# Four side-by-side products of 32 output columns in place of one of 128 in a softmax attention

## What is computed

```
qkv = (x @ W_qkv + b_qkv).reshape(B, S, 3, H, hd)
q, k, v = (qkv[:, :, 0], qkv[:, :, 1], qkv[:, :, 2])
attn = jnp.einsum('bqhd,bkhd->bhqk', q, k) / jnp.sqrt(jnp.asarray(hd, x.dtype))
attn = jax.nn.softmax(attn, axis=-1)
attn_out = jnp.einsum('bhqk,bkhd->bqhd', attn, v).reshape(B, S, D)
```

## Time and profile before

| | us |
|---|---|
| median of three runs | 2016.27 (2015.23 to 2020.01) |
| the profiled execution, device time | 2018.79 |
| its span in the profile | 2017.1 |
| PE busy | 1833.6 (91%), 10746 matmuls |
| DVE busy | 1480.3 (73%) |
| ACT busy | 939.5 (47%) |
| POOL busy | 965.1 (48%) |
| `pass_attend` | about 1563 to 2016 |

### The profile page before, as it was taken

How to read it: one execution, slowest core, us unless ns; L and a number is a source line. 1 busy time by engine, 2 the same in 40 slices (tenths; PEclk the granted TensorE clock), 3 DMA queues, 4 the chain that set the end, 5 groups by cost and what they waited for, 6 DMA issues and landing times. The chain is left out here.

```text
span 2017.1 us, 36263 instructions
## 1 busy us (share of the span) xinstructions
PE 1833.6 (91%) x10746; PEld 1204.9 (60%) x10746; DVE 1480.3 (73%) x4020; ACT 939.5 (47%) x2132; POOL 965.1 (48%) x1658
## 2 busy tenths in 40 slices
PE   6997997999899999799999699599799699999997
PEld 5886774444688888577777333388677233333332
DVE  3334896777477777699998498577798589998981
ACT  1112564666121121344443244355444477777777
POOL 3554564666333333233333111088743776666663
PEclk9997998999799999899999799699899699999999
DMA  4330668887100000695000200067786344443320
GB/s 134 117 117 27 163 167 207 162 173 144 48 1 1 1 1 1 270 413 232 1 1 1 65 10 10 29 157 200 193 254 204 69 107 101 102 106 92 88 68 28
DMA packets 241706, 215.01 MB, mean 107 GB/s; under 512 B 117210, under 2 KB 216188, under 8 KB 241404
## 3 DMA queue, kind: packets, MB, share of 16 engines
q1 hardware_dynamic: 227804, 183.51, 34.1%
q0 software_dynamic: 9408, 25.70, 3.9%
q10 hardware_dynamic: 4320, 3.70, 0.7%
HBM read 108.04 MB, written 103.12 MB: 105 GB/s over the span
## 5 line engine op out<-in xcount | busy, mean ns | idle before, releaser
L2918 ACT ACTIVATE attend_w<-ps 128x512 f32<-128x512 f32 x512 | 279.9, 598 | 91.2 <-PE ps L2785 67.1
L3121 DVE TENSOR_REDUCE attend_mx<-ps 128x1 f32<-128x512 f32 x448 | 281.7, 682 | 36.1 <-PE ps L2773 26.5
L2785 PE MATMUL ps<-keep_o,keep_x 99*128 99x512 bf16 x512 | 191.9, 384 | 2.4 <-ACT attend_w L2918 2.4
L2773 PE MATMUL ps<-keep_x,keep_o 96*128 96x512 bf16 x448 | 173.3, 387 | 8.0 <-DVE attend_mx L3121 6.3
L987 POOL TENSOR_TENSOR keep_early<-keep_early,first_causal 128x128 f32<-128x128 f32 x256 | 110.9, 456 | 77.7 <-ACT keep_early L961 76.7
L1009 DVE SCALAR_TENSOR_TENSOR keep_early<-ps,first_causal 128x512 f32<-128x512 f32 (+3 forms) x256 | 111.4, 486 | 44.8 <-PE ps L901 44.0
L2803 PE MATMUL ps<-attend_w,keep_early 128*17 128x512 f32 x1024 | 136.0, 600 | 0.0
L1215 PE MATMUL ps<-mlp_zT,keep_early 128*128 128x128 f32 x1056 | 128.2, 280 | 8.0 <-ACT mlp_zT L1257 8.0
L961 ACT ACTIVATE keep_early<-ps 128x512 f32<-128x512 f32 (+3 forms) x256 | 97.0, 435 | 74.6 <-PE ps L901 74.0
L1215 PEld LDWEIGHTS ps<-mlp_zT,keep_early 128*128 128x128 f32 x1056 | 121.9, 194 | 16.0 <-ACT mlp_zT L1257 16.0
L2773 PEld LDWEIGHTS ps<-keep_x,keep_o 96*128 96x128 bf16 x448 | 43.8, 98 | 144.9 <-DVE attend_mx L3121 105.1
(11 more groups left out here) (405 smaller groups left out, 4483.1 us busy)
## 6 DMA issues: line engine op xcount, KB each, us to landing
sorted<-keep_x SPq DMA_DIRECT2D x3, 14720.0 KB, 75.2
tok_xin<-in_xk SPq DMA_DIRECT2D x64, 256.0 KB, 2.6
qk_parts<-qkv_parts SPq DMA_DIRECT2D x33, 384.0 KB, 3.2
qk_parts<-moe_parts SPq DMA_DIRECT2D x32, 384.0 KB
sorted<-moe_zn POOLq DMA_DIRECT2D x64, 128.0 KB, 3.2
moe_zs<-sorted SPq DMA_DIRECT2D x45, 128.0 KB, 3.2
keep_o<-qk_parts SPq DMA_DIRECT2D x14, 384.0 KB, 4.4
keep_x<-qk_parts SPq DMA_DIRECT2D x14, 384.0 KB, 5.6
```

Source lines behind the costliest of these rows:

```text
L2773: nc.tensor.matmul(ps[:, bank, :], qs[0:R, x.buf(0), h, t * P:(t + 1) * P], ks[0:R, x.buf(0), h, :], start=True, stop=True).then_inc(s_msc, 1)
L2785: nc.tensor.matmul(ps[:, SC + i % RING, :], ks[:, x.buf(2), HG * g + j, kt * P:(kt + 1) * P], qs[:, x.buf(2), HG * g + j, :], start=True, ...
L2918: nc.scalar.activation(w[:, j, kt % 2, :], ps[:, SC + (HG * k + j) % RING, :], ACT.Exp)\
L3121: nc.vector.tensor_reduce(mx[:, t, k:k + 1], ps[:, MX + (at + 1) % RING, :], AX, ALU.max)\
```

## The change

`max_scores`, `scores` and `class_values` issue each product of 128 output columns as four of 32 output columns. Each has its own columns of the weights, the same streamed data (512 columns), the same bank, its own 32 output partitions and its own quarter of the array (`tile_position=(0, 32 * q)`). The semaphore is raised by the last of the four. The class row's values (now `ps[0:8]`, 8 weight columns) and its sum (now `ps[0:1]`, one weight column) shrink to the output that is read, with as many matmuls as before. pT becomes a quarter of a size and is no longer cleared, since no zero columns are read any more.

```diff
@@ pass_attend
+    QUAD = 2 * HD
-        pT = a.sb("pT", [P, TB, P // HALF, HALF])
+        pT = a.sb("pT", [P, TB, HALF])
@@ on PE
+            def product(bank, keys, queries):
+
+                for q in range(P // QUAD):
+                    cols = slice(QUAD * q, QUAD * (q + 1))
+                    last = nc.tensor.matmul(ps[cols, bank, :], keys[:, cols], queries, start=True, stop=True,
+                                            skip_group_check=True, tile_position=(0, QUAD * q))
+                return last
@@ max_scores
-                nc.tensor.matmul(ps[:, bank, :], qs[0:R, x.buf(0), h, t * P:(t + 1) * P], ks[0:R, x.buf(0), h, :],
-                                 start=True, stop=True).then_inc(s_msc, 1)
+                product(bank, qs[0:R, x.buf(0), h, t * P:(t + 1) * P], ks[0:R, x.buf(0), h, :]).then_inc(s_msc, 1)
@@ scores
-                nc.tensor.matmul(ps[:, SC + i % RING, :], ks[:, x.buf(2), HG * g + j, kt * P:(kt + 1) * P],
-                                 qs[:, x.buf(2), HG * g + j, :], start=True, stop=True).then_inc(s_sc[j], 1)
+                product(SC + i % RING, ks[:, x.buf(2), HG * g + j, kt * P:(kt + 1) * P], qs[:, x.buf(2), HG * g + j, :])\
+                    .then_inc(s_sc[j], 1)
@@ class_values
-                    nc.tensor.matmul(ps[:, CTX, :], vb[:, b, half, 2 * HD * HG * g:2 * HD * HG * (g + 1)],
-                                     cwp[:, half, :], start=True, stop=False, skip_group_check=True)
+                    for q in range(P // QUAD):
+                        cols = slice(QUAD * q, QUAD * (q + 1))
+                        nc.tensor.matmul(ps[cols, CTX, :], vb[:, b, half, 2 * HD * HG * g + QUAD * q:2 * HD * HG * g + QUAD * (q + 1)],
+                                         cwp[:, half, :], start=True, stop=False, skip_group_check=True, tile_position=(0, QUAD * q))
@@ side_work, k == 5 and k == 7
-                        last = nc.tensor.matmul(ps[:, MISC, 0:VW], pT[:, t, :, :].rearrange("p a h -> p (a h)"), v[:, x.buf(1), t, :],
+                        last = nc.tensor.matmul(ps[0:HALF, MISC, 0:VW], pT[:, t, :], v[:, x.buf(1), t, :],
-                    nc.tensor.matmul(ps[:, MISC, 0:VW], env.ones[:, :], t1[:, 1, :, :].rearrange("h g d -> h (g d)"),
+                    nc.tensor.matmul(ps[0:1, MISC, 0:VW], env.ones[:, 0:1], t1[:, 1, :, :].rearrange("h g d -> h (g d)"),
@@ ACT, k == 4
-                        nc.scalar.copy(pT[:, :, 0, :], ps[:, MISC, 0:TB * HALF].rearrange("p (t h) -> p t h", h=HALF))\
+                        nc.scalar.copy(pT[:, :, :], ps[:, MISC, 0:TB * HALF].rearrange("p (t h) -> p t h", h=HALF))\
@@ DVE, head of the pass
-            nc.vector.memset(pT[:, :, :, :], 0.0)
```

## The result

| | before | after |
|---|---|---|
| median | 2016.59 us | 2039.74 us (2032.6 to 2041.98) |
| ratio | | 1.0106, 95% interval 1.0077 to 1.0136 |
| profiled execution, span | 2017.1 us | 2036.1 us |
| PE matmuls | 10746 | 13722 |
| one softmax unit | 27.15 us | 28.0 us, with 34.0, 30.9, 29.5 and 29.5 among them |

The forecast was 2010.4 us, faster by 0.3%; the time lies 12 us above the range.

What follows compares the result with a forecast made beforehand. PE was taken to bound about 17.6 us of each 27.2 us unit, DVE the rest. Savings of 4.3 (14 units) + 1.2 (last slots) + 0.4 (head) = 5.9 us from 2016.27 made 2010.4 us; range 2001 to 2028.

Steps and rivals of the forecast that it cites:

- Product spacing and feeding in general: Score, maximum and class-value products: four of 32 columns come 0.22 us apart, as one whole product did; no change.
- Value visits: Changes into and out of value products at k=1 to k=5: 0.20 us saved each, 1.00 us a unit.
- Transposes: 128-column side work at k=1, k=2 and k=6: new mode changes lose 0.23 us each, 0.69 us a unit.
- The small transposes at step 4: 8-row transposes at k=4, already 0.31 us behind their product: pay a mode change before and after, so 0.
- The DVE part: About 9.5 us at a unit's end where PE waits for DVE: 0.60 us saved at k=6, 7 and 0 stays hidden.
- rival A: Gain lands in all eight steps of a unit, 0.91 us each unit: 2002.0 us; chance 0.13.
- Last slots: Last two slots, without maxima: seven plain steps save 0.18 us each, 1.2 us together (between 0 and 2.9).
- Head: Start of the stage: no longer clearing pT, which stood in the chain ahead of `prod`, saves 0.4 us.
- Waits and queues: No wait added or moved, no transfer touched; DVE and ACT see a product about 0.02 us later.
- C: PE cannot be fed eight instructions in 0.22 us per product: 2057 us, or 2028 halfway; chance 0.19.
- B: Side-work visits at 0.34 us each eat the unit's gain, leaving 1.6 us: 2014.7 us; chance 0.23.
- D: The four parts of a product don't run side by side, costing up to 0.88 us a product: 2600 us; chance 0.03.

Runs made afterwards that it cites:

- e8: The kernel before with four plain DMAs in place of POOL's indirect ones, gather by position left out: 2011.43 us (0.9979).
- e7: The changed kernel with four plain DMAs in place of POOL's indirect ones, gather by position left out: 2006.91 us (0.9952); again on another chip 2008.91 us (0.9950).
- e20: The changed kernel with score products and class values of steps 5 and 6 whole (128 columns), fours in the other six steps: 2026.37 us (1.0044).
- e21: The changed kernel with products in fours only in steps 5 and 6, whole products in the other six: 2029.37 us (1.0056).
- e2: The kernel before with only the class row's two products narrowed: 2022.17 us (1.0004).
- r1: The changed kernel itself, run again on a fourth chip beside plain, split and early fetches: 2047.99 us (1.0144).
- e9: The changed kernel with all four indirect fetches moved to the slot's start: 2020.35 us (1.0024) on one chip, 2056.91 us (1.0182) on another.
- e10: The changed kernel with two of four indirect fetches moved to the slot's start: 2012.38 us (0.9984) on one chip, 2042.13 us (1.0103) on another.
- e3: The changed kernel with the class row's narrow products issued in every quarter of the array: 2055.78 us (1.0168).

## Why the prediction was wrong, point by point

To read it step by step I took the time from one signal of the value products to the next, out of the same record of semaphores (median of the ordinary units, us; the first and last column run from and to `largest`):

```
                     ->0   0->1  1->2  2->3  3->4  4->5  5->6  6->7  7->    unit
before              2.09   4.32  3.27  2.83  3.28  3.98  3.27  3.07  1.05  27.15
after               1.98   3.90  3.30  2.66  3.40  6.12  2.63  2.87  1.15  28.02
e8 (whole, plain)   2.09   3.49  3.27  2.83  3.28  3.98  3.27  3.07  1.05  26.33
e7 (fours, plain)   1.98   3.64  3.30  2.66  3.40  3.78  3.51  2.84  1.00  26.11
e20                 1.98   4.45  3.30  2.66  3.40  4.17  3.27  3.06  0.95  27.25
e21                 2.09   3.49  3.27  2.83  3.28  5.95  2.64  3.25  1.05  27.85
```

**Product spacing and feeding in general: right.** 0.22 us for four, so 27 ns an instruction can be fed for as long as POOL doesn't issue indirect DMAs. The 62 ns a matmul that the prediction cited from the Trainium skill (TensorE: Matmul & The Clock Gate, "Wait — 56ns, not 53.3ns?") would be 0.25; the rows show 0.22, and it doesn't bind.

**Value visits: right.** 0.20 a visit; e7 less e8 gives 0.17 at 2->3 and 0.20 at 4->5, where nothing else changes.

**Transposes: right in size at two of three.** Forecast, net of the value visit, +0.03 in steps 1 and 2, and +0.23 in step 6, whose value visit was counted as hidden. Measured (e7 less e8) +0.15, +0.03 and +0.24.

**The small transposes at step 4: wrong.** Forecast 0, since they already stood 0.31 behind their product. Then 3->4 should have fallen by 0.20; it rose by 0.12. PE's timeline of the kernel after, at step 4:

```profile
1800.25 0.39 PE L2771 MATMUL ps<-keep_o,keep_x 99*32 99x512 bf16 x4
1800.94 0.38 PE L2844 MATMUL ps<-keep_ident,attend_pc 8*128 8x8 f32 x4 [0.31 <-ACT attend_pc L2908]
```

They stand 0.69 behind the product and wait for ACT's exponential of the class row. The 0.31 that the prediction read as a change of mode had PE and ACT arrive almost together: the transposes start 0.14 us behind the end of ACT's exponential now, and started 0.18 behind it before. What PE gained in the steps before, it gives back there. That is the question it did not ask: when a stall goes, what is late next?

**The DVE part: partly wrong.** The visits of steps 7 and 0 were counted as hidden. They brought 0.23, 0.05 and 0.11: some of rival A was true. The errors nearly cancel, which was luck: 0.22 us a unit where 0.31 was forecast, over 14 units 1.3 of the 1.4 us between 4.5 and 5.9, closer than the medians can tell. They don't cancel in e20, which pays at steps 1 and 4, pays 0.19 for the change of mode at step 5, and has none of the gain at steps 5 and 7.

**Class row: right.** Narrowing costs nothing (e7 less e8 at 4->5 is the value visit's 0.20 and no more; e2, 1.0004). **Last slots: right.** They gained 1.40 us, and 1.26 in e7 against e8 (forecast 1.2). **Head: can't be told.** It gained 0.33 in the same pair (forecast 0.4) and lost 0.78 in the first, while it scatters from 21.9 to 25.0 between runs.

**The step that failed** is the paragraph "Waits and queues": "No wait is added or moved", "No transfer is touched", and so nothing beside PE was looked at. True of the program, not of the chip. While POOL issues indirect DMAs, PE's signals for products in fours mostly come 0.74 us apart. A whole product, 2 instructions for its 0.22 us, isn't held; in fours it has 8. At step 5 that costs 2.34 us (6.12 against 3.78), of which step 6 gives back 0.88; four products at 0.22 had passed ahead of their signals, and they would make just that. With 0.03 in step 7 and 0.15 at the end of the unit, 1.64 us. From that come off the 0.22 of gain and 0.57 by which, at the start of the unit, DVE now meets POOL less (4.32 less 3.90 is 0.42, plus the 0.15 that the transposes cost there). Left are 0.85 of the 0.87 us measured for an ordinary unit. The twelve units behind the first two make 13.6 us of the 23.0, and the first two, with the hold at steps 7 and 0 and the lower clock, 9.4.

**The rivals.** C, that PE cannot be fed, named the right kind of limit and the wrong place for it: it was priced as one rate for all of the stage, "from 27 ns on", at 2028 or 2057 us with a chance of 0.19. The rate is met everywhere but in 5 us of 27, and there signals come at a third of it. The result lies between its two prices. A is true of half of its steps. B, the visits of the side work at 0.34, fell: they cost 0.24. D fell.

Not in any case: the long units. A hold leaves PE idle for 2 us or more, and the granted clock can then fall: once in a while in the profiled run of the kernel after, in nearly every unit of r1 (30.57 us, 0.94). Why the hold is longer on r1's chip (2.25 us at the class row against 1.5) these runs don't say.

**Open.** Why PE's signals are late while POOL issues indirect DMAs and not while it issues plain ones; whether the products themselves are late or only their signals; whether plain fetches spare PE by their kind or by their shorter issue (2.17 us of POOL for four, against 3.87); and why e9 and e10 were spared on one chip. No kernel with all of the computation beat the kernel before on a chip with the hold; e10 did by 0.16%, on the one where none was seen.

## What to carry to other kernels

Before an instruction is split, look beside it, not only ahead and behind: which engine issues indirect DMAs, when, and how many instructions the split puts into those microseconds. A price taken from a quiet stretch holds for quiet stretches. And PE's rows show when a matmul started and what its end should be; when others could use its result shows only in its signal and in when its waiters start.

A cure seen on one chip, beside the illness seen on another, is not a cure. Run the ill kernel beside it, on the same chip.

## What the runs showed of the hardware

- While POOL issues indirect DMAs (4 of 0.96 us each, 128 rows) beside products in fours, most of PE's signals come in steps of about 0.74 us: 8 instructions (four loads and four matmuls) 0.74, 16 instructions 1.46, the 64 of e3's class row 3.77, which is less than in proportion; some follow at 0.06. Beside whole products, 16 instructions of values signal 1.01 us behind the product before them and on time. The hold sets in up to 1.4 us behind the first issue. Seen on four chips and in the first run of the changed kernel, in every variant with indirect fetches beside fours; not seen in e9 and e10 on one further chip. With plain DMAs of the same bytes: never, on two chips.
- Small matmuls of one quarter let the other three quarters run ahead: three quarters of a product started at 1805.13, the fourth at 1805.48, ahead of matmuls that stand earlier in the program.
- A DVE operation that reads two operands from SBUF and meets one of POOL's takes about as long as that one: 0.74 us for 0.19. Here it cost the kernel before 0.83 us in an ordinary unit, more than the change was to gain.
